# Four pairs of quads' own products in 12 units a tile instead of 16, operands put together by ScalarE, and no DMA halving early in the first tile

## What is computed

```python
e = jnp.stack([tbl_0[ids[:, 0]], ..., tbl_31[ids[:, 31]]], axis=1)   # 2048 x 32 x 64
p = e[:, ids_x, :]                       # first field of each of the 496 pairs
q = e[:, ids_y, :]                       # second field
pw = jnp.einsum('bpi,pij->bpj', p, w)    # w: 496 x 64 x 64
z = jnp.einsum('bpj,bpj->bp', pw, q)
h = jnp.concatenate([z, dense_ctx], axis=1)          # 512 wide
h = jnp.maximum(h @ W_top1 + b_top1, 0.0)            # 512
h = jnp.maximum(h @ W_top2 + b_top2, 0.0)            # 256
y = h @ W_top3                                       # 1
```

## Time and profile before

| | us |
|---|---|
| median of 3 runs | 858.94 (858.76 to 859.58) |
| profiled execution, first to last instruction (its span) | 856.9 |
| median less span | 2.0 |
| PE busy | 782.8 |
| DVE busy | 592.4 |
| POOL busy | 574.1 |
| ACT busy | 195.7 |

### The profile page before, as it was taken

How to read it: one execution, slowest core, us unless ns; L and a number is a source line. 1 busy time by engine, 2 the same in 40 slices (tenths; PEclk the granted TensorE clock), 3 DMA queues, 4 the chain that set the end, 5 groups by cost and what they waited for, 6 DMA issues and landing times.

```text
span 856.9 us, 10445 instructions
## 1 busy us (share of the span) xinstructions
PE 782.8 (91%) x3912; PEld 287.9 (34%) x3912; DVE 592.4 (69%) x512; ACT 195.7 (23%) x333; POOL 574.1 (67%) x597
## 2 busy tenths in 40 slices
PE   0467739998989999999999999999999999999998
PEld 0122213333333333333333333333333333333333
DVE  0145528977877768868689677877788677887750
ACT  1222202131222132311322222311322223200002
POOL 6777775778777777777787777777777777710100
PEclk9969969999999999999999999999999999999999
DMA  4524539969797887888697986888786988994820
GB/s 131 203 52 100 122 78 197 218 156 200 167 199 166 182 187 158 191 181 173 152 203 157 204 182 139 196 184 182 140 204 161 200 195 189 193 187 92 167 56 0
DMA packets 38601, 138.07 MB, mean 161 GB/s; under 512 B 11092, under 2 KB 11476, under 8 KB 28056
## 3 DMA queue, kind: packets, MB, share of 16 engines
q0 software_dynamic: 28048, 101.75, 60.3%
q1 hardware_dynamic: 10504, 35.67, 12.2%
HBM read 52.43 MB, written 0.01 MB: 61 GB/s over the span
## 4 chain that ended last, share of the span: by engine, by line
PE 76%; POOL 13%; issue 5%; DMA 5%; DVE 1%; ACT 0%; POOLq 0%; DVEq 0%
PE main_ps L332 44%; PE z_ps L355 17%; POOL emb L233 12%; PE x_ps L386 8%; PE x_ps L312 4%; DMA prod<-prod 4%; PE main_ps L386 2%; POOL prod L245 1%; DMA emb<-in_tbl,idx 1%; DVE prod L419 1%; PE main_ps L333 1%; ACT quad_t L442 0%; DMA idx<-in_ids 0%; ACT y_sb L465 0%; POOLq L230 0%
## 5 line engine op out<-in xcount | busy, mean ns | idle before, releaser
L419 DVE TENSOR_TENSOR prod<-main_ps,quad_t 128x1024 f32<-128x1024 f32 x448 | 521.8, 1217 | 151.8 <-PE main_ps L333 151.3
L233 POOL DMA_INDIRECT emb<-in_tbl,idx x512 | 494.0, 965 | 165.4 <-issue 149.2
L332 PE MATMUL main_ps<-e_t,w_sb 64*128 64x512 f32 x1024 | 488.6, 617 | 4.1 <-ACT e_t L431 4.1
L333 PE MATMUL main_ps<-e_t,w_sb 64*128 64x512 f32 x1024 | 488.6, 617 | 0.0
L332 PEld LDWEIGHTS main_ps<-e_t,w_sb 64*128 64x128 f32 x1024 | 185.0, 191 | 260.8 <-issue 184.3
L355 PE MATMUL z_ps<-prod,const_sb 128*32 128x512 f32 x1400 | 177.4, 604 | 28.3 <-DMA prod<-prod 26.1
L333 PEld LDWEIGHTS main_ps<-e_t,w_sb 64*128 64x128 f32 x1024 | 185.0, 191 | 0.0
L419 DVE TENSOR_TENSOR prod<-main_ps,e_t 128x1024 f32<-128x1024 f32 x64 | 78.1, 1220 | 83.8 <-PE main_ps L333 83.8
L442 ACT ACTIVATE quad_t<-x_ps 32x512 f32<-32x512 f32 x224 | 131.2, 586 | 2.7
L245 POOL DMA_DIRECT2D prod<-prod x81 | 80.0, 993 | 74.0 <-DVE prod L419 69.3
L431 ACT ACTIVATE e_t<-x_ps 128x512 f32<-128x512 f32 x64 | 38.2, 597 | 400.0 <-PE x_ps L312 400.0
(11 more groups left out here) (11 smaller groups left out, 24.3 us busy)
## 6 DMA issues: line engine op xcount, KB each, us to landing
prod<-prod POOLq DMA_DIRECT2D x81, 1024.0 KB
w_sb<-in_w SPq DMA_DIRECT2D x65, 512.0 KB, 5.8
emb<-in_tbl,idx POOLq DMA_INDIRECT x512
w_sb<-in_w SPq DMA_DIRECT2D x1, 1024.0 KB, 11.9
z_sb<-in_ctx SPq DMA_DIRECT2D x64, 2.0 KB
idx<-in_ids SPq DMA_DIRECT2D x1, 192.0 KB, 9.6
const_sb<-in_const SPq DMA_DIRECT2D x1, 125.0 KB, 2.2
idx<-in_ids SPq DMA_DIRECT2D x1, 64.0 KB, 1.9
```

The costliest lines, as they stand in the source:

```text
L233: pool.indirect_dma_start(out=emb[:, n % G_SLOTS, s, odd * EMBED:(odd + 1) * EMBED], out_offset=None, in_=tables[f], in_offset=bass.Indire ...
L332: nc.tensor.matmul(main_ps[:, slot, :], w_sb[LOW, u % W_SLOTS, :], even[LOW, 0, :], start=True, stop=True)
L333: nc.tensor.matmul(main_ps[:, slot + 1, :], w_sb[UP, u % W_SLOTS, :], odd[UP, 0, :], start=True, stop=True)\
L419: nc.vector.tensor_tensor(prod[:, s:s + 2, :], main_ps[:, slot:slot + 2, :], e_q, ALU.mult)\
```

## The change

The units of quads' own products are put together differently. Two quads form a "star": 3 units whose halves take different fields, with the second operands picked from two duos. Four stars replace the 8 pieces, so a tile has 28 rounds of 4 units and 4 rounds of 3 units (rounds 2, 7, 18 and 29), 124 units instead of 128. The second operands of a star need features of two duos side by side: ACT puts them together in four new slots of `e_t` by 4 copies of 64 partitions for each quad (`mix_quad`), 32 copies a tile, and DVE waits for them.

All rounds but the star rounds can be folded; which are is listed in `UNFOLDED`. The first tile folds none of its first 24 rounds. There are 77 folds: 7, 24, 24 and 22 by tile (before: 20, 20, 20 and 21).

POOL's rule for gathers is new. During the first 24 rounds it issues gathers up to 6 duos ahead of the transposes. After that a running goal counts the gathers, 136 plus 4 for each round, and whatever a duo's transposes still lack is issued at the duo's place in the list. The unfolded rounds have no wait on POOL any more. The rounds of the duos' transposes (`STEADY`) and of the MLP steps (`MLP_AT`) are new, too. The 16 dense numbers of a tile now come in 8 DMAs instead of 16, into rows of all four `z` tiles, the last among them; PE's first MLP matmul waits for them and for the last `z` tile. The options for half-wide tiles in the new code are not used: all four widths are 512.

```diff
-def ahead(n):
-
-    return 2 if n < 10 else 3 if n < DUOS else G_SLOTS
...
+def order_groups():
+    low = []
+    for m in range(13, 1, -1):
+        low += [(m, q) for q in range(QUADS - 1, m // 2, -1)]
+    low += [(m, q) for q in range(QUADS - 1, 0, -1) for m in (1, 0)]
+    groups = [("low", low[k:k + 2]) for k in range(0, len(low), 2)]
+    for at, q in ((2, 7), (7, 5), (18, 3), (29, 1)):
+        groups.insert(at, ("star", (q, q - 1)))
...
+def star_units(qa, qb):
+
+    a, b = [4 * qa + k for k in range(4)], [4 * qb + k for k in range(4)]
+    return [((a[2], (a[0], a[1])), (a[1], (a[0], a[3]))),
+            ((b[0], (b[2], b[3])), (b[1], (b[0], b[3]))),
+            ((b[2], (b[1], b[3])), (a[3], (a[0], a[2])))]
...
+UNFOLDED = {0: range(24), 1: (6, 14, 22, 28), 2: (6, 14, 22, 28), 3: (6, 14, 22, 28, 30, 31)}
+FOLDS = [(t, r) for t, r in ROUNDS if foldable(t, r) and r not in UNFOLDED[t]]
...
+STEADY = (-6, -4, -3, -1, 0, 2, 3, 4, 7, 9, 11, 13, 15, 18, 20, 22)
+DUO_AT = {1: STEADY, 2: STEADY, 3: STEADY}
+MLP_AT = {t: (5, 9, 13, 17, 21, 25, 29) for t in (1, 2, 3)}
...
-DUO_ROUNDS = (-9, -7, -5, -3, -1, 1, 3, 5, 7, 9, 11, 13, 15, 17, 19, 21)
-MLP_ROUNDS = (6, 10, 14, 18, 22, 26, 30)
...
+            n = max(FIRST_DUO[t][m] - 1, 0) if t == 0 else min(STEP0[ROUND0[t] + DUO_AT[t][j]], FIRST_DUO[t][m])
+            at[m] = max(n, at.get(m + 1, 0))
+            put(at[m], ("duo", t, m))
...
+        for q in range(QUADS - 1, -1, -1):
+            g = STAR_GROUP[q if q % 2 else q + 1]
+            star = g if WIDTHS[t] == FULL else g // 2
+            lead = (2 if WIDTHS[t] == FULL else 0) + q % 2
+            put(max(STEP0[max(ROUND0[t] + star - lead, 0)], at[2 * q]), ("mix", t, q))
         if t:
-            for n, r in enumerate(MLP_ROUNDS):
-                due.setdefault(t * NUNIT + ROUND * r, []).append(("mlp", t - 1, n))
...
+FREE_ROUNDS, FREE_GATHERS = 24, 136
...
-                if n >= ahead(n) and k == 0:
-
-                    pool.wait_ge(transposed, n - ahead(n) + 1)
+                if n >= G_SLOTS and k == 0:
+
+                    pool.wait_ge(transposed, n - G_SLOTS + 1)
...
-            todo = [(n, k) for n in range(TILES * DUOS) for k in range(2 * SUBS)]
-            seen = 0
-            for kind, t, n in EVENTS:
+            todo = [(n, k) for n in range(TILES * DUOS) for k in range(gathers(n // DUOS))]
+            total, seen = len(todo), 0
+            for kind, a, b in EVENTS:
                 if kind == "duo":
-                    seen = duo_number(t, n) + 1
-                elif kind == "unit" and n % ROUND == ROUND - 1:
-                    paced = t > 0 or n > 10 * ROUND
-                    room = len([g for g in todo if g[0] < seen + ahead(g[0])])
-                    for _ in range(min(room, POOL_GATHERS) if paced else room):
+                    while todo and todo[0][0] <= duo_number(a, b):
                         gather(*todo.pop(0))
-                    if (t, n // ROUND) in FOLDS:
-                        fold(t, n // ROUND)
-                    elif paced:
-
-                        pool.wait_ge(products, NUNIT * t + n + 1)
-                        pool.nop(nofuse=True)
+                    seen = duo_number(a, b) + 1
+                elif kind == "end":
+                    goal = total if a < FREE_ROUNDS else min(total, FREE_GATHERS + 4 * (a + 1 - FREE_ROUNDS))
+                    while total - len(todo) < goal and todo[0][0] < seen + G_SLOTS:
+                        gather(*todo.pop(0))
+                    if ROUNDS[a] in FOLDS:
+                        fold(a)
...
+                    for i, g in enumerate(STARS):
+                        k, rr, _ = z_place(a, g)
+                        if k != b:
+                            continue
+
+                        sp.wait_ge(z_out, Z0[a] + k + 1)
+                        c = 0 if WIDTHS[a] == FULL else HALF * (g % 2)
+                        for x in range(2):
+                            row, f = z_row(rr, 3, x, 0, True), 4 * i + 2 * x
+                            sp.dma_start(z_sb[row:row + 2, a % 2, k, c:c + WIDTHS[a]],
+                                         ctx_t[f:f + 2, FIRST_COL[a]:FIRST_COL[a] + WIDTHS[a]]).then_inc(ctx_in, 16)
...
+                        if n == 0 and k == 0:
+                            pe.wait_ge(z_out, Z0[t + 1])
...
+                if kind == "star":
+                    if ps[0] == 0:
+                        dve.wait_ge(mixed, MIXED["mix", t, what[1]])
+                    for h, p in enumerate(ps):
+                        c = slice(HALF * (g % 2), HALF * (g % 2) + HALF) if WIDTHS[t] == HALF else slice(0, FULL)
+                        a = prod_tile(G, p, 0)
+                        ins = nc.vector.tensor_tensor(prod[:, a:a + 2, c], main_ps[:, slot:slot + 2, HALF * h:HALF * h + WIDTHS[t]],
+                                                      star_operand(t, *what, p), ALU.mult)
...
+            def mix_quad(t, q):
+                first, pair = q % 2 == 1, q if q % 2 else q + 1
+                act.wait_ge(evicted, EVICTED["duo", t, 2 * q])
+
+                if pair < QUADS - 1:
+                    act.wait_ge(products, FINAL_STAR[t][pair + 2] + 1)
+                elif t:
+                    act.wait_ge(products, FINAL_STAR[t - 1][1] + 1)
+                a, b = e_duo(t, 2 * q), e_duo(t, 2 * q + 1)
+                one, other = (mix(t, 0), mix(t, 3)) if first else (mix(t, 1), mix(t, 2))
+                nc.scalar.activation(one[LOW, :], a[LOW, :], ACT.Copy)
+                nc.scalar.activation(one[UP, :], b[UP, :], ACT.Copy)
+                if first:
+                    nc.scalar.activation(other[LOW, :], a[LOW, :], ACT.Copy)
+                    last = nc.scalar.activation(other[UP, :], b[LOW, :], ACT.Copy)
+                else:
+                    nc.scalar.activation(other[LOW, :], a[UP, :], ACT.Copy)
+                    last = nc.scalar.activation(other[UP, :], b[UP, :], ACT.Copy)
+                last.then_inc(mixed, 1)
```

More of the change, by code:

```diff
@@ L43 @@
[L43 to L68, removed]
+def order_groups():
[6 more added lines that the diff above has]
+        groups.insert(at, ("star", (q, q - 1)))
+    return groups
@@ L81 @@
[L81 to L98, removed]
-                    ctx += 1
[L100 to L104, removed]
-    return rows
@@ L139, in order_events @@
-    ev += [("reduce", TILES - 1, ROUNDS - k) for k in range(PAST, 0, -1)] + [("z", TILES - 1, KTILES - 1)]
+    for G, (t, r) in enumerate(ROUNDS):
+        for k in range(len(steps_of(t, r))):
+            ev += due.get(STEP0[G] + k, [])
+            ev.append(("step", G, k))
+        ev.append(("end", G, 0))
+        if G >= PAST:
+            ev.append(("reduce", G - PAST, 0))
+            pt, pr = ROUNDS[G - PAST]
+            if pr % ROUNDS_KT == ROUNDS_KT - 1:
+                ev.append(("z", pt, pr // ROUNDS_KT))
@@ new lines, in reduce_round @@
+                if len(set(kinds)) == 1:
+                    spans = [(kinds[0], slice(0, FULL))]
+                else:
+                    spans = [(kind, slice(HALF * c, HALF * c + HALF)) for c, kind in enumerate(kinds)]
+                todo = []
+                for p in range(2 if folded else 4):
+                    for kind, c in spans:
+                        if kind == "low" or p < 3:
+                            todo += [(p, x, kind, c) for x in range(2)]
+                for i, (p, x, kind, c) in enumerate(todo):
+                    q = 2 * (p % 2) + x
+                    if kind == "low":
+                        lhs = sel_quad[:, 28 - 4 * rr:60 - 4 * rr]
+                    else:
+                        s = 2 * rr + (p >= 2)
+                        lhs = sel_duo[:, 30 - 2 * s:62 - 2 * s]
+                    final = not any(2 * (pp % 2) + xx == q for pp, xx, _, _ in todo[i + 1:])
+                    last = nc.tensor.matmul(z_ps[32 * q:32 * q + 32, c], lhs, prod[:, prod_tile(G, p, x), c],
+                                            start=(rr == 0 and p < 2), stop=(rr == ROUNDS_KT - 1 and final))
```

495 lines of the change are left out of this document (300 added, 195 removed).

## The result

The changed kernel takes 1171.38 us (median, 1170.21 to 1173.38) beside 858.96 of before in the same runs: 1.3638 times as long, 95% interval 1.3618 to 1.3657. The prediction was 1154, range 1085 to 1205. The profiled execution spans 1168.5 us.

The account below looks back on a forecast made before the run. Tile 0 was taken as bound by gathers, tiles 1 to 3 by TensorE, with GpSimd full as well. Terms: 247 + 553.1 + 237.3 + 17.4 + 64.4 + 33 = 1152.2, with 2.0 outside the span 1154 us; range 1085 to 1205.

Parts of the forecast that it names:

- end of tile 0: First tile: ends at 247 us, taken between 238 if nothing waits and 257 if nothing is gained.
- TensorE's work in tiles 1 to 3, full clock: Tiles 1 to 3: fewer units and cheaper reductions take 17.9 us off 571.0, leaving 553.1.
- waits for gathered rows there: Tiles 1 to 3: TensorE waits before transposes for late gathers, 80.9 us a tile, 75.5 in tile 1, 237.3 in all.
- MLP steps behind evictions: Rounds 9 and 13: MLP step right behind a duo's transposes waits 2.9 us for their eviction, six times, 17.4 us.
- clock: TensorE in tiles 1 to 3: slower matmuls after each of 23 waits over 5 us, 2.8 us each, 64.4 us.
- tail: After the last tile's products: 29 us become 33, as dense rows go into the last z tile after its copy.
- Where gathers stand between folds: GpSimd's queue, tiles 1 to 3: gathers stand behind folds that wait for products, so transposes wait; 237.3 us.
- lead 0: Duos 4 and 5 of a tile: gathers neither ahead of nor short of the need; 5.4 us of wait each.
- 11 over 9.5: From a round's last unit to the gathers' landing: 11 us taken; less a 1.0 us reduction, 10.0 of wait.
- The rival by which the clock recovers at once: TensorE in tiles 1 to 3: clock loss 0 in place of 64.4, time 1090; chance 0.13.
- Stars: TensorE: four units less save 3.43 us a tile; reductions fall from 42.2 to 38.8 us in tiles 1 and 2.
- The other side (faster, 835): Tiles 1 to 3: gathers early enough, some two rounds ahead of transposes, so nothing is lost; 835 us, chance 0.04.

Follow-up runs that it names:

- e5: Changed kernel with the goal of gathers at 152 instead of 136 and MLP steps at rounds 6, 10, 14, 17, 21, 25, 29: 840.93 us.
- e1: Changed kernel with the goal of gathers starting at 152 instead of 136, nothing else: 867.82 us.
- e3: Kernel before, with only the change's rule for gathers (goal of 136 plus 4 a round from round 24 on): 1352.59 us.
- e7: Changed kernel, TensorE filling the waits before the transposes of duos 7 to 12 of tiles 1 to 3 with matmuls: 1223.33 us.
- e6: Changed kernel with MLP steps at rounds 6, 10, 14, 17, 21, 25, 29, where none meets transposes; gathers as they are (136): 1127.35 us.
- e12: e5 with no folds in the first 26 rounds of the first tile instead of 24: 834.32 us, the fastest of all.
- e9: e7 with about half as many filling matmuls (13, 7, 8, 8, 9 and 8): 1155.71 us.
- e4: Changed kernel with MLP steps at rounds 6, 10, 14, 18, 22, 26, 30; 18 and 22 are rounds of transposes too: 1171.18 us.
- e11: Kernel before without folds in the first 24 rounds of its first tile, nothing else of the change: 838.56 us.

## Why the prediction was right

The mechanism was right, and so was nearly every term (us):

| term | predicted | measured | where |
|---|---|---|---|
| end of tile 0 | 247 | 246.4 | after |
| TensorE's work in tiles 1 to 3, full clock | 553.1 | 553.7 | e5 |
| waits for gathered rows there | 237.3 | 254.1 | after |
| MLP steps behind evictions | 17.4 | 17.7 | after |
| clock | 64.4 | 617.9 - 553.7 = 64.2 | after, e5 |
| tail | 33 | 32.3 | after |
| outside the span | 2.0 | 1170.4 - 1168.5 = 1.9, in the profiled execution (the median is 0.9 more) | after |

- **Where gathers stand between folds.** Shown by one number in either kernel (e1, e3). The mis-sized term is the waits': 16.8 us too little, which is nearly all of the miss of 17. The duos 4 and 5 (lead 0) waited 6.1 to 7.9 instead of 5.4, two of the last three 2.4 to 3.8 instead of 1.5 (the third did not wait), duo 11 11.1 to 11.4 instead of 10.0; duo 6 waited 1.0 to 2.5 instead of 4.3. For duos 9 and 10 the 10.0 held (9.8 to 10.6), and so did the reason that made me choose 11 over 9.5: the gathers end behind the fold. Duo 11 of tile 1: the fold and the last gather in the chain, then the time from the issue of this one fold to its landing:

```profile
388.59 1.01 POOL prod L350
...
393.79 3.03 DMA emb<-in_tbl,idx
```

```profile
DMA to landing us min/median/max: 7.4/7.4/7.4
```

The fold landed at 396.0, the gather at 396.8. At 22 of the 34 waits the last gather went out some 5.2 us behind a fold, and each time it landed behind that fold, by 0.6 to 2.6 us; at the other 12 it went out some 10 us behind one, the fold had landed before, and the gather took 2.3 to 2.6. The sum of 10.0 is partly luck all the same. The fold took 7.4 to 7.8 us to land ahead of the duos 9 to 11 where I had 8.67, and the gather followed 0.7 to 0.8 behind it where I had 1.5; against that, a gather still to be issued when the products came kept the fold in the chain further above for 0.95 us, and the reduction beside that wait is one of 1.9 us, not of 1.0 (9.84 + 1.91 = 11.75, where I had 10.0 + 1.0). At the duos of lead 0 another fold was issued 0.95 us behind the last gather; there the fold ahead took 8.3 to 9.1 us to land and the gather followed 1.8 to 2.6 behind it, 10.4 to 11.2 in all from the fold's issue, where my 11 has 9.0 for this. That stretch is what was too small.

- **The clock.** The sum was right, and e1 and e7 show that the waits cause it. Its parts were not right: a filled wait cost 2.4 where I had 2.8, and the 21.2 us that are left (64.2 - 43.0) belong to the other waits, of which I had counted five. That these two misses cancel is luck. The rival by which the clock recovers at once is out. The Trainium skill, "TensorE: Matmul & The Clock Gate", What's actually happening, puts the ramp under 1% of a typical kernel's span; the loss behind this kernel's repeated waits is 64.2 of 1168.5, 5.5%, and the measurement decides. Its section HAM oscillation, on waits for DMA after each of which the engine starts throttled anew, agrees with this trace: the granted clock is 0.83 to 0.84 in each of the three tiles.
- **The MLP steps.** The size was right, but e6 shows that their place was worth 44 us, not 17.4: I counted what the step waits for, not what it could cover.
- **Stars.** Four units less a tile and cheaper reductions were sized to within 1 us (553.1, measured 553.7); ScalarE's copies cost nothing that shows.
- **Tile 0.** 247 came out by luck. I took it halfway between 238 (nothing waits) and 257 because I could not tell; the 238 was right, as e12 shows with 238.6. The difference to 246.4 is that the first folds did hold reductions up (8.1 us in two waits), where I had written that they hold little up.
- **The other side (faster, 835)** needed gathers some two rounds ahead. With 16 more of them and the MLP steps moved, 840.9 was measured, and 834.3 with two folds fewer in tile 0: its condition was right, and its price to within 6 us.

## What to carry to other kernels

When one in-order queue issues two kinds of work, of which one waits for results and the other feeds them, count for each fed item which waiting instruction stands just ahead of it: within a round of its use, the ring from result to feed lies bare on the path, and 16 places in the queue were worth 300 of 1171 us here. Look at both sides, since too much lead makes the other kind late. Before a wait that can't be removed, place independent work of about its length; work placed right behind it pays the wait's clock as well.

## What was not expected of the hardware

- A gather issued 5.2 us behind a fold landed behind it at all 22 waits of this kind in tiles 1 to 3. I had expected the order, but not how far it spreads: 3.0 to 3.3 us after its own issue where no other fold followed within that time, 3.7 to 6.05 where one was issued 0.9 to 2.2 us behind it. What sets the spread isn't settled.
- Filling waits by matmuls gave 43.0 us of TensorE's time back in e7, but only 14.6 in e9, where rests of 2.3 to 3.7 us were left; and an MLP step behind transposes that had waited for 7.83 us took 6.53 us instead of 3.63 (e4).
- 14 reductions of twice the matmuls in tile 0 of the old kernel cost 7.8 us of TensorE's time and saved 25.6 us of its waiting (e11).
